# A hybrid block on one core: 24 instead of 21 shared tiles ahead of the routed ones, the choice tables spread over twelve steps, and the routed rows of twelve tiles added to X by accumulating transfers

## The reference

```python
logits = jnp.einsum('th,eh->te', x, gate_w)                      # E = 8
topk_w, topk_i = jax.lax.top_k(softmax(logits), 2)               # two experts a row
topk_w = topk_w / jnp.sum(topk_w, axis=-1, keepdims=True)
eo = jnp.einsum('eti,eih->eth', silu(g) * u, w_down)             # I = 352
out = jnp.einsum('te,eth->th', combine, eo)
sg = sigmoid(jnp.einsum('th,oh->to', x, shared_gate_w))
so = silu(x @ sw_gate) * (x @ sw_up) @ sw_down
x = x + out + sg * so
```

## Time and profile before

| | |
|---|---|
| median of 3 runs | 1965.76 us (1962.02 to 1970.11) |
| profiled execution, its own time | 1961.4 us |
| its span | 1959.6 us |
| mean granted clock of PE | 0.984 |
| PE, DVE, ACT busy | 95%, 69%, 59% of the span |
| end of moe1's routed rows to attention's first instruction | 615.8 to 657.3 us |
| end of moe2's routed rows to the end | 1914.8 to 1959.6 us |

### The profile page before, as it was taken

One profiled execution on the slowest core, in us unless ns is written; L12 is line 12 of the kernel. 1 busy time (PEld: TensorE's weight loads), 2 busy tenths in 40 slices (PEclk: granted clock), 3 DMA queues, 4 the chain that ended last, 5 costly groups with the idle time before them and its releaser, 6 DMA issues. The chain is left out here.

```text
span 1959.6 us, 51770 instructions
## 1 busy us (share of the span) xinstructions
PE 1863.6 (95%) x19842; PEld 1443.2 (74%) x19842; DVE 1359.9 (69%) x2732; ACT 1161.8 (59%) x2351; POOL 404.2 (21%) x490
## 2 busy tenths in 40 slices
PE   6999899999999888899999999999998999999998
PEld 5677688999999654465555555565545789999997
DVE  6555668644445778899999999999953778444446
ACT  5211344444444453699989898999995534444442
POOL 1121100455552142000000000000000001555540
PEclk9999989999999899999999999999999999999999
DMA  7000121122225475421212111111004311222227
GB/s 301 1 1 0 43 66 31 57 78 77 79 76 176 133 187 147 109 50 41 49 49 54 47 43 41 41 41 41 3 3 193 95 46 28 76 79 78 74 84 279
DMA packets 85771, 151.75 MB, mean 77 GB/s; under 512 B 35876, under 2 KB 68004, under 8 KB 79332
## 3 DMA queue, kind: packets, MB, share of 16 engines
q1 hardware_dynamic: 71884, 110.06, 18.7%
q0 software_dynamic: 13632, 38.41, 6.3%
q10 hardware_dynamic: 24, 0.02, 0.0%
HBM read 99.30 MB, written 48.76 MB: 76 GB/s over the span
## 5 line engine op out<-in xcount | busy, mean ns | idle before, releaser
L2153 ACT ACTIVATE att_scores_pt<-att_scores_psE 128x512 f32<-128x512 f32 x1024 | 598.1, 597 | 68.5 <-PE att_scores_psE L1655 26.3
L1670 DVE TENSOR_REDUCE att_mx<-att_scores_psS 128x1 f32<-128x1024 f32 x472 | 577.9, 1224 | 49.9 <-PE att_scores_psS L1655 18.6
L1655 PE MATMUL att_scores_psE<-att_qs,att_ks 99*32 99x512 bf16 x4096 | 437.5, 382 | 3.9 <-DVE att_scores_psO L2183 3.2
L2255 PE MATMUL att_scores_psO<-att_scores_pt,att_va 128*17 128x256 f32 x4096 | 330.2, 379 | 2.9 <-ACT att_scores_osb L2158 1.3
L1655 PE MATMUL att_scores_psS<-att_ks,att_qs 96*32 96x512 bf16 x3776 | 308.5, 380 | 0.1
L1655 PEld LDWEIGHTS att_scores_psE<-att_qs,att_ks 99*32 99x32 bf16 x4096 | 136.1, 95 | 103.7 <-ACT att_scores_pt L2153 8.8
L2255 PEld LDWEIGHTS att_scores_psO<-att_scores_pt,att_va 128*17 128x17 f32 x4096 | 131.5, 98 | 103.2 <-issue 13.3
L819 PE MATMUL moe_ps<-W_rest,moe_srcT_high 128*128 (+2 forms) x824 | 201.2, 325 | 0.0
L280 POOL DMA_INDIRECT work<-normalised_rows,moe_slots_i x142 | 138.3, 974 | 271.7 <-DVE moe_slots_i L604 227.4
L623 DVE TENSOR_TENSOR moe_hidT_rest<-moe_ps,moe_hidT_high 128x384 fp32r<-128x384 f32 x142 | 79.1, 557 | 156.6 <-ACT moe_hidT_high L353 156.6
L1655 PEld LDWEIGHTS att_scores_psS<-att_ks,att_qs 96*32 96x32 bf16 x3776 | 126.1, 97 | 78.0 <-issue 1.3
(11 more groups left out here) (318 smaller groups left out, 3150.7 us busy)
## 6 DMA issues: line engine op xcount, KB each, us to landing
work<-expert_rows SPq DMA_DIRECT2D x16, 1024.0 KB, 4.7
W_gate_up<-in_gate_up_dram SPq DMA_DIRECT2D x2, 6346.0 KB, 21.8
query_key_parts<-att_qkv_parts SPq DMA_DIRECT2D x64, 192.0 KB, 3.1
normalised_rows<-work SPq DMA_DIRECT2D x64, 128.0 KB, 1.8
work<-normalised_rows SPq DMA_DIRECT2D x56, 128.0 KB, 2.1
att_qs<-query_key_parts SPq DMA_DIRECT2D x16, 384.0 KB, 4.3
att_ks<-query_key_parts SPq DMA_DIRECT2D x16, 384.0 KB, 4.4
W_down<-in_down_a_dram SPq DMA_DIRECT2D x2, 2304.0 KB, 28.3
```

The source lines that it names most:

```text
L1655: last = nc.tensor.matmul(out[j:j + 32, :], stationary[:, j:j + 32], moving, start=True, stop=True, tile_position=(0, j), skip_group_check ...
L1670: return nc.vector.tensor_reduce(a.mx[g % 2][:, v:v + 1], bank[:, :, :].rearrange("p h k -> p (h k)"), AX.X, ALU.max)
L2153: nc.scalar.activation(pt[s % 2][:, r, :], psE[use % E_BANKS][:, :], ACT.Exp, scale=HD ** -0.5).then_inc(p_ready, 1)
L2255: last = nc.tensor.matmul(psO[32 * r:32 * r + VC, cols], va[g][:, kt, r * VC:(r + 1) * VC], pt[s % 2][:, r, cols], start=(kt == 0 and part ...
```

## The change

- `NA` goes from 21 to 24: three more shared tiles stand ahead of the routed steps and three fewer (8) behind. The number of steps is the same.
- `one_hots` is split into `hot_lanes`, `hot_blocks` and `hot_tiles`, and `tables(n)` does two pieces in three steps: 8 pieces over steps 8 to 19. `slots` moves from step 17 to 20, `block_experts` from 16 to 10, the final `choice_weights` from step 8 to 9, and the zeroing of its buffer `cw` from DVE to POOL. ACT's `lanes` and PE's `inverse` follow by `column_step` and `index_step`.
- Twelve tiles (groups 0 to 2, `BY_DMA` = 3) are no longer fetched to `got` and added by DVE. POOL issues six transfers, one for each group and each of the two results, 512 KB each, that add rows of `expert_rows` to X in SBUF (`accum_op`). They begin when all results are stored and the second fetch has landed, and transfers on the same group wait for each other through `added`.
- SP fetches five groups instead of eight, and waits for all six adding transfers before it stores the output in moe2, or leaves the phase in moe1.
- In moe1's step 31 DVE takes `bn_stats` of tiles 0 to 3 only. Attention takes those of tiles 4 to 7, between `rows_rest(0)` and `weights_rest`, and the `bn_aggr` of these tiles moves there as well.

The core of the diff:

```diff
-NA = LOOK + 17
+NA = LOOK + 20
...
+        BY_DMA = 3
...
-        FOUND = LOOK + 4 + CH // PIECE + 1
+        TABLES = LOOK + 4
+        FOUND = TABLES + CH // PIECE * 3 // 2
+        column_step = lambda i: TABLES + i // 2 * 3 + i % 2 * 2
+        index_step = lambda i: TABLES + i // 2 * 3 + 1 + i % 2
...
-            for g in range(GOT):
+            for g in range(BY_DMA, BY_DMA + GOT):
                 rows_of(g)
             late_rows(LATES + 2)
-            for g in range(GOT, FOURS):
-                if LATES + g < NT - NA:
-                    late_rows(LATES + g)
-                rows_of(g)
-            for l in range(LATES + FOURS, NT - NA):
-                late_rows(l)
+            late_rows(LATES + 3)
+            rows_of(BY_DMA + GOT)
+            late_rows(LATES + 4)
+            rows_of(BY_DMA + GOT + 1)
+            for g in range(BY_DMA):
+                sp.wait_ge(added[g], 16 * TOPK)
...
+            def add_rows(g, k):
+
+                tiles = slice(g * GS, (g + 1) * GS)
+                pool.dma_start(X[:, tiles, :], results[:, tiles, k, :], accum_op=ALU.add).then_inc(added[g], 16)
+
+            for u in range(SRC):
+                pool.wait_ge(y_sent[u], sent_by(u))
+            pool.wait_ge(d_used, BY_DMA * GS)
+            pool.wait_ge(got_loaded[1], 16)
+            add_rows(0, 0)
+            add_rows(1, 0)
+            pool.wait_ge(added[0], 16)
+            add_rows(0, 1)
+            pool.wait_ge(added[1], 16)
+            add_rows(1, 1)
+            pool.wait_ge(added[0], 32)
+            add_rows(2, 0)
+            pool.wait_ge(added[2], 16)
+            add_rows(2, 1)
...
+            def tables(n):
+
+                q, part = divmod(n - TABLES, 3)
+                if part == 0:
+                    hot_lanes(2 * q)
+                    hot_blocks(2 * q)
+                elif part == 1:
+                    hot_tiles(2 * q)
+                    hot_lanes(2 * q + 1)
+                else:
+                    hot_blocks(2 * q + 1)
+                    hot_tiles(2 * q + 1)
+                if n == TABLES + 1:
+                    choice_weights()
+                if n == TABLES + 2:
+                    block_experts()
...
                 if t == NT - 1:
-                    dve.wait_ge(by_dve, FOURS)
+                    dve.wait_ge(by_dve, FOURS - BY_DMA)
                     if out is None:
-                        for first in range(2 * GS):
+                        dve.wait_ge(added[0], 16 * TOPK)
+                        for first in range(GS):
                             row_stats(first)
...
-            spreads(slice(CT, 2 * CT))
             for u in range(2):
                 for j in range(CT):
                     nc.vector.memset(vt[u][j][:, :, HD:VC], 1.0)
             rows_rest(0)
+            for t in range(CT, 2 * CT):
+                nc.vector.bn_stats(stats[:, t, :], X[:, t, :])
+            dve.drain()
+            spreads(slice(CT, 2 * CT))
```

More of the change, by code:

```diff
@@ L168, in ffn_phase @@
         got_loaded = [sem(f"got_loaded{g}") for g in range(GOT)]
-        by_dve = sem("by_dve"); out_stored = sem("out_stored")
+        by_dve = sem("by_dve"); added = [sem(f"added{g}") for g in range(BY_DMA)]; cw_zero = sem("cw_zero"); out_stored = sem("out_stored")
         LAST = NA + NB
@@ L183, in ffn_phase @@
                       FOUND + 1: range(4, 7), FOUND + 2: range(7, 10), FOUND + 3: range(10, 12)}
-        SPLIT_REST = {FOUND - 1: range(0, 1), FOUND: range(1, 3), FOUND + 1: range(3, 6), FOUND + 2: range(6, 9),
-                      FOUND + 3: range(9, 12)}
+        SPLIT_REST = {TABLES + 5: range(0, 1), TABLES + 8: range(1, 2), TABLES + 11: range(2, 3),
+                      FOUND + 1: range(3, 6), FOUND + 2: range(6, 9), FOUND + 3: range(9, 12)}
         def down_piece(i):
@@ L225, in rows_of @@
             def rows_of(g):
-                if g >= GOT:
-                    sp.wait_ge(by_dve, g - GOT + 1)
-                sp.dma_start(got[g % GOT][:, :, :, :], results[:, g * GS:(g + 1) * GS, :, :]).then_inc(got_loaded[g % GOT], 16)
+                q = g - BY_DMA
+                if q >= GOT:
+                    sp.wait_ge(by_dve, q - GOT + 1)
+                sp.dma_start(got[q % GOT][:, :, :, :], results[:, g * GS:(g + 1) * GS, :, :]).then_inc(got_loaded[q % GOT], 16)
             for l in range(LATES + 2):
@@ L245, in _ @@
                     end = min((g + 1) * GS, NT - 1)
-                    sp.wait_ge(by_dve, g + 1)
+                    if g >= BY_DMA:
+                        sp.wait_ge(by_dve, g - BY_DMA + 1)
                     sp.wait_ge(d_used, end)
@@ L270, in _ @@
                            allow_small_or_imprecise_dtypes=True).then_inc(consts_done, 1)
+            pool.wait_ge(hot_ready, 1)
+            nc.gpsimd.memset(cw[:, :, :], 0.0).then_inc(cw_zero, 1)
             def fetch(j):
@@ L390, in step @@
                     extra_out(n * BESIDE + 1)
-                if 0 <= here - LOOK - 6 < CH // PIECE:
-                    lanes(here - LOOK - 6)
+                for i in range(CH // PIECE):
+                    if here == column_step(i) + 2:
+                        lanes(i)
                 silu_step(n, n % 2)
@@ L491, in choice_weights @@
             def choice_weights():
-                nc.vector.memset(cw[:, :, :], 0.0)
-                dve.drain()
+                dve.wait_ge(cw_zero, 1)
                 dve.wait_ge(cw_done, 1)
@@ L569, in positions, with hot_lanes, hot_blocks @@
                 dve.drain()
-            def one_hots(i):
-                c = slice(i * PIECE, (i + 1) * PIECE)
-                over = lambda v, n: v[:, c, None].to_broadcast([P, PIECE, n])
+            choices = lambda i: slice(i * PIECE, (i + 1) * PIECE)
+            over = lambda v, i, n: v[:, choices(i), None].to_broadcast([P, PIECE, n])
+            def hot_lanes(i):
+                if i >= 2:
+                    dve.wait_ge(inv_done, i - 1)
+                nc.vector.tensor_tensor(hot_p[i % 2][:, :, :], iota_p[:, None, :].to_broadcast([P, PIECE, P]),
+                                        over(pos_p, i, P), ALU.is_equal)
+            def hot_blocks(i):
                 if i:
@@ L646, in combine @@
             def combine(g, shared_added):
-                at, t = got[g % GOT], g * GS
-                dve.wait_ge(got_loaded[g % GOT], 16 * (g // GOT + 1))
+                q, t = g - BY_DMA, g * GS
+                at = got[q % GOT]
+                dve.wait_ge(got_loaded[q % GOT], 16 * (q // GOT + 1))
                 nc.vector.tensor_tensor(at[:, :, 0, :], at[:, :, 0, :], at[:, :, 1, :], ALU.add)
@@ L712, in _ @@
             source_rest(1, 1)
-            finding = {LOOK: choose_first, LOOK + 1: lambda: choose(1), LOOK + 2: counts, LOOK + 3: positions,
-                       FOUND - 1: block_experts, FOUND: slots}
+            finding = {LOOK: choose_first, LOOK + 1: lambda: choose(1), LOOK + 2: counts, LOOK + 3: positions, FOUND: slots}
             for n in range(NA):
-                i = n - LOOK - 4
-                if i == 0:
-                    choice_weights()
-                step(n, "shared", finding.get(n, (lambda: one_hots(i)) if 0 <= i < CH // PIECE else None))
+                step(n, "shared", finding.get(n, (lambda: tables(n)) if TABLES <= n < FOUND else None))
             for n in range(NA, LAST):
@@ L925, in step @@
                     rows_in(n + 1, buffer(here + 1), nk, loaded)
-                if LOOK + 6 <= here < LOOK + 6 + CH // PIECE:
-                    inverse(here - LOOK - 6)
+                for i in range(CH // PIECE):
+                    if here == index_step(i) + 2:
+                        inverse(i)
                 if here == LOOK + 3:
```

13 lines of the change are left out of this document (6 added, 7 removed).

## The result

The changed kernel takes 1992.26 us (median of four executions, 1989.36 to 1996.74), the kernel before 1963.89 us (1956.25 to 1970.11) beside it: a ratio of 1.0148, 95% interval 1.0106 to 1.0191. It is slower, by 28 us where 19 were forecast. The profiled execution took 1996.74 us with a span of 1995.0 us, 35.4 us more than the span of before.

A forecast was written before the change was run, and what follows sets the result against it. PE was taken to bound the kernel, busy 1863.6 of 1959.6 us, with moe2's end set as much by DMA traffic. The terms 13.4 + 4.1 + 1.5 + 0 gave +19.0 us, hence 1983 us, range 1969 to 1999.

The forecast's parts named there:

- adds at 2 to 3.4 us: Main case: each add takes the DMA engines 2 to 3.4 us, the kernel +12 to +28 us; chance 0.57.
- The end of moe2: Last stores wait behind the adds, ending at t0 (first fetch) + 45.5 against 32.1: +13.4 us (+6.3 to +18.3).
- I take 2.5 us, two reads at the 420 GB/s of the large transfers: Engine time assumed for one 512 KB add, between bounds of 1.7 and 3.4 us.
- The start at t0 + 1.3: At moe2's end, the engines' 28.4 us of fetches, late tiles and adds begin about 1.3 us after the first fetch.
- The end of moe1: SP leaves the phase only after all six adds, at t0 + 33.1 against 29.0: +4.1 us (-1.4 to +9).
- Attention: Four moved statistics, a drain and an aggregate stand ahead of weights_rest, so PE comes +1.5 us later (0 to +1.8).
- The table steps: Spreading inverse gains nothing; 0.5 us hidden in a stall, some 0.6 lost in step 10: together 0 (-1 to +1).
- the rival on the faster side: DVE paces the table steps, so 16 steps fall to 3.80 us, giving 8.8 back; chance 0.05 together with no effect.
- The late tiles: The late tile behind three fetches also shares engines with two adds: 1 to 2 us more PE idle per layer, hidden.
- One rival: An add costs far more than two reads, 5 us each: moe1 pays 17, moe2 26, about 2010 us; chance 0.08.
- All 4.19 MB now stand behind the adds: At moe2's end all output stores follow the adds, taking 10.0 us at 420 GB/s and 2.4 for issue and landing.
- The rival that rested on the Trainium skill's fit for POOL's transfers: An add costs about a plain copy and the chain hides: +5 to +9 us, 1971 to 1975; chance 0.30.

The follow-up runs named there:

- plain_copies: The changed kernel with its six transfers a stage copying rows over X instead of adding them, all waits kept; 1969.47 us, ratio 1.0044.
- adds_alone: The kernel before with only the six adds per stage, no tiles moved ahead, old tables and eight statistics; 1972.04 us, ratio 1.0059.
- the filled kernels: Filler products in each expert stage's first step, added to the kernel before (1955.33 us, ratio 0.9979) and to the changed kernel (1999.44 us, ratio 1.0140).
- stores_first: The changed kernel with SP storing the groups that DVE adds before it waits for the adding transfers; 1989.79 us, ratio 1.0142.
- no_adds: The changed kernel without POOL's adding transfers and the waits for them, those routed rows left out of the result; 1956.77 us, ratio 0.9989.

## Why the prediction was right in kind and 9 us short

**The main mechanism held.** No time was won by moving tiles, the adds end behind PE, SP stands behind them and every store follows. The case "adds at 2 to 3.4 us" came in just above its upper end (3.45), and the time, 1992.3 us, in the range of 1969 to 1999. Between the medians lie 28.4 us, the upper edge of the main case; between the profiles 35.4, beyond the +30 of the sum. Two of its terms left their own ranges, the end of moe1 and attention. Of the 35.4 us 19.0 were forecast; the rest is:

- **The end of moe2, +13.4 forecast, +16.9 measured** (50.8 against 44.8 - 10.9), inside +6.3 to +18.3. The step that failed is "I take 2.5 us, two reads at the 420 GB/s of the large transfers": an add measured 3.45 us (20.7 / 6). The doubling was right, the base was not. A copy of this shape takes 1.5 us, not 1.25, the addition doubles that to 3.0, and the stride adds 0.5 (on the average). Six times 0.95 us is 5.7, and the stores began 4.6 us later than forecast. The row to take was the earlier trace rows: its 1.7 us for a copy, doubled, was the 3.4 that stood as the upper bound. That this comes so near is in part luck: 1.7 is the rate of indirect transfers, the copy took 1.5, and the cut into rows, which the prediction had no term for, makes up the difference. The 2.4 us of a bare wait held, though the earlier trace rows is no tiny transfer's row but that of a scatter of 128 rows of 1 KB. The start at t0 + 1.3 rests on a return of 0.9 us that no row gives; the trace of before shows the engines at work from t0 + 0.9.
- **The end of moe1, +4.1 forecast, +10.5 measured** (41.2 against 41.6 - 10.9), above the +9 that was the bound. The same term: the last add, issued at 656.26, lands at t0 + 38.0 instead of 33.1. (That it is 6.4 over and not 6.8 with the next point comes from the shift, 10.9 and not 11.4.) Another 1.9 us lie between that landing and attention's start, 3.1 against 1.2 before. In plain_copies it is 3.1 us too, so it isn't the addition; adds_alone, where DVE ends last, has 1.2. Which of the barrier's parts takes them no run shows. DVE was done long before, at t0 + 30.0 (t0 + 29 was forecast), as the row ahead of the barrier shows.

DVE in the changed kernel at that place, answering to the earlier trace rows:

```profile
652.22 1.41 DVE L711 BATCH_NORM_STATS2 stats<-X 128x6 f32<-128x256 f32 x4
653.55 0.47 DVE L697 SCALAR_TENSOR_TENSOR X<-moe_ps,moe_sg,X 128x256 f32<-128x256 f32 x1
665.25 0.38 DVE L1955 BATCH_NORM_AGGREGATE att_qkv_mv<-stats 128x2 f32<-128x6 f32 x4 [11.23 <-PEq L47]
...
672.63 1.26 DVE L1987 TENSOR_TENSOR Wqk_rest<-Wqk,att_qkv_wqk_high 128x512 fp32r<-128x512 f32 x2
```

- **Attention, +1.5 forecast (0 to +1.8), +3.4 measured.** PE's timeline, answering to the earlier trace rows:

```profile
665.25 2.04 PE L53 MATMUL att_qkv_ps<-ones 128*128 128x512 f32 x2 [11.76 <-PEq L47]
...
673.35 1.40 PE L2073 MATMUL att_qkv_ps<-att_qkv_xT,Wqk_rest 128*128 128x512 f32 x2 [1.29 <-DVE Wqk_rest L1987]
```

  The wait for `Wqk_rest` is there at 1.3 us. PE had stood idle for 11.8 us where it was 3.1 before, and its first two products took 2.04 us where before's took 1.18. The next tiles come 1.8 us later in all. The remaining 1.6 us lie elsewhere in the stage; the same code differs by more between these runs (adds_alone, with attention as before, takes 881.1 us where the kernel before takes 878.4), so I leave it open.
- **The table steps, 0 forecast, about half a microsecond a stage gained.** Steps with `inverse` last 4.35 us, those without 3.8. PE in the second stage, answering to the earlier trace rows:

```profile
1632.19 1.51 PE L920 MATMUL moe_ps<-W_down,work 128*128 128x256 f32 x6
1636.04 0.66 PE L826 MATMUL moe_ps<-work 128*128 128x144 bf16 x8
1636.54 1.51 PE L920 MATMUL moe_ps<-W_down,work 128*128 128x256 f32 x6
1640.38 1.46 PE L920 MATMUL moe_ps<-W_down,work 128*128 128x256 f32 x6
...
1678.69 1.56 PE L920 MATMUL moe_ps<-W_down,work 128*128 128x256 f32 x6 [0.67 <-ACT work L381]
```

  The stall behind `slots` fell from 1.22 to 0.67, the 0.5 that was forecast. The loss of 0.6 in step 10 didn't come, so the two don't cancel; this is the 0.5 by which the shift above is 10.9 and not 11.4. That DVE set the pace of these steps, the rival on the faster side, fell.
- **The late tiles** wait as forecast, by 1 to 2 us more in each layer (2.3 us in moe1 and 2.8 in moe2, before 0.2 and 1.3), hidden by the adds, which end later:

```profile
PE moe_ps L792 <- DMA work<-normalised_rows: 5.1, 4, 2.5
```

- **What had no term:** +2.1 us in the fronts beyond the three tiles, which is the clock to within 0.2 us (3.5 + 8.7 us lost to it in the changed kernel, 8.8 + 1.1 before, by the filled kernels), and +2.5 us ahead of the first expert stage, where the code is the same. With 3.5, 6.4 and 1.9 from the three terms above that makes the 16.4 missing of 35.4, to rounding.

The medians differ by 28.4 us, not 35.4: the profiled execution of the changed kernel is the slowest of its four, 4.5 us above their median, and that of the kernel before lies 2.5 us below its own. With four executions of each I can't split the 28.4 further. One rival was summed too low: by the prediction's own sum six adds of 5 us end at t0 + 48.1, not t0 + 46.

**The step that misled in its emphasis** was "All 4.19 MB now stand behind the adds". It reads as if the order of SP's queue were the loss. stores_first shows that it isn't: with the stores ahead the end is 0.6 us sooner only, because fetches, adds and stores fill the same engines for up to 46 of 51 us. The rival that rested on the Trainium skill's fit for POOL's transfers (DMA: Bandwidth & Descriptors, Anatomy of one DMA) fell: its estimate is 3.2 us from issue to landing, and a bare copy here landed after 3.8 at least, a bare add after 5.7. The prediction took the fit to be for plain copies; the page names no kind of transfer. The same page's rule that all issuers share the 16 engines is what stores_first bears out: with SP's stores beside them the adds came later.

## What to carry to other kernels

Price a transfer that accumulates at twice the engine time of a copy of the same shape, as a first estimate (measured here for one size, 512 KB of float32 from HBM into SBUF), and somewhat more if it is cut into 1 KB rows; take that copy's rate from the share of the queue that will carry it, not from the largest transfers of another. Before handing work to a DMA queue, add up what must pass the engines from the first of these transfers to the end: where that sum is near the stretch's length, order gives back little (0.6 us by stores first, 4 to 5 by three adds at once), and the work that covered the traffic must not be moved away in the same change. Take a stage's own landmark (here the first gather) to separate a clock that fell from work that was added.

## What the runs showed of the hardware

- An accumulating transfer of 512 KB from HBM into SBUF takes 3.0 us of all 16 engines with 4 KB contiguous per partition, 3.45 us from 1 KB rows, against 1.5 for a copy (averages of six; the last, which runs alone, takes 3.4, 3.5 and 1.6); alone it lands after 5.7 us at least in both forms, a copy after 3.8; POOL is held 0.85 and 1.27 us for its issue, against 0.75.
- A copy of 1 KB rows showed 144 packets whether its target was contiguous or strided, an add from 1 KB rows 528, an add from 4 KB pieces 144.
- The granted clock falls to 0.50 (1.2 GHz) in the first steps of an expert stage, in 17 of 22 profiled stage starts, for some 3 us (the kernel before, second stage) to some 24 us (its first stage). Ahead of the fall PE waits twice for nearly 1 us (0.92 for DVE and 0.97 for ACT in the changed kernel's second stage); the same waits stand in no_adds's second stage, where the clock stayed at 1.00. With filler products in these waits it stayed at 1.00 in all four stage starts of two kernels, and the kernel before was faster, 0.9979 (0.9961 to 0.9997).
